# A q/k item split by ScalarE and VectorE straight from its PSUM bank, with the items' products spread in another way

## The reference

```python
mod = silu(condition) @ Wada + bada
sh_a, sc_a, gt_a, sh_m, sc_m, gt_m = jnp.split(mod, 6, axis=1)
xm = layernorm(x, g1, be1) * (1.0 + sc_a[:, None, :]) + sh_a[:, None, :]
q, k, v = split_heads(xm @ Wqkv)
attn = softmax(where(causal, q @ k.T * scale, -inf))
x = x + gt_a[:, None, :] * ((attn @ v) @ Wproj + bproj)
xm = layernorm(x, g2, be2) * (1.0 + sc_m[:, None, :]) + sh_m[:, None, :]
x = x + gt_m[:, None, :] * (gelu(xm @ W1 + b1) @ W2 + b2)
```

## Time and profile before

| | |
|---|---|
| median of 3 runs | 3148.65 us (3148.61 to 3149.07) |
| the profiled execution | 3149.18 us |
| its span, first to last instruction | 3147.5 us |
| mean granted TensorE clock | 0.999 |
| TensorE matmuls busy | 98% of the span |
| VectorE, GpSimd, ScalarE busy | 78%, 54%, 45% |

### The profile page before, as it was taken

How to read it: one execution, slowest core, us unless ns; L and a number is a source line. 1 busy time by engine, 2 the same in 40 slices (tenths; PEclk the granted TensorE clock), 3 DMA queues, 4 the chain that set the end, 5 groups by cost and what they waited for, 6 DMA issues and landing times.

```text
span 3147.5 us, 64741 instructions
## 1 busy us (share of the span) xinstructions
PE 3099.2 (98%) x22888; PEld 2417.4 (77%) x22888; DVE 2451.6 (78%) x2975; ACT 1429.7 (45%) x2876; POOL 1704.9 (54%) x1385
## 2 busy tenths in 40 slices
PE   8999999999999999999899999999999999999999
PEld 5677777777777777766688888888888888888888
DVE  5688887787888778766787878878787787878874
ACT  4355555555555555566543333333333333333333
POOL 3388888888888888888742323232322322323232
PEclk9999999999999999999999999999999999999999
DMA  7666566666656666676713222221222313222120
GB/s 251 211 191 193 170 193 183 177 188 184 194 174 187 183 177 187 181 192 178 180 41 81 57 63 68 52 80 46 74 57 63 79 41 80 57 63 67 53 67 14
DMA packets 304625, 391.81 MB, mean 124 GB/s; under 512 B 24296, under 2 KB 206088, under 8 KB 304448
## 3 DMA queue, kind: packets, MB, share of 16 engines
q1 hardware_dynamic: 292336, 371.86, 41.7%
q10 hardware_dynamic: 12112, 17.42, 1.6%
HBM read 270.66 MB, written 118.00 MB: 123 GB/s over the span
## 4 chain that ended last, share of the span: by engine, by line
PE 90%; DVE 5%; issue 2%; DMA 1%; ACT 1%; POOL 1%; SPq 0%; DVEq 0%; ACTq 0%; POOLq 0%
PE psY L1025 22%; PE psH L1013 14%; PE psA L793 9%; PE psT L847 9%; PE psH L1016 7%; PE psA L885 7%; PE psA L797 6%; PE psP L922 6%; PE psS L816 4%; DVE mx L1379 2%; PE psA L858 2%; PE psA L765 1%; DVE psS L1375 1%; PE psA L907 1%; PE psA L902 1%
## 5 line engine op out<-in xcount | busy, mean ns | idle before, releaser
L1654 POOL TENSOR_TENSOR h_l<-h_full,h_h 128x256 fp32r<-128x256 f32 x512 | 451.2, 881 | 1099.5 <-ACT h_h L1255 1099.5
L1117 ACT ACTIVATE e<-psT 128x512 f32<-128x512 f32 (+1 forms) x1202 | 605.6, 555 | 377.0 <-PE psT L847 373.6
L1379 DVE TENSOR_REDUCE mx<-psS 128x4 f32<-128x2048 f32 (+3 forms) x384 | 665.9, 1755 | 118.6 <-PE psS L816 80.5
L1252 ACT ACTIVATE h_full<-h_full,b1c 128x256 f32<-128x256 f32 x512 | 260.4, 509 | 995.1 <-DVE h_full L1555 995.1
L1013 PE MATMUL psH<-a_l,w1p_h 128*128 128x512 f32 x2048 | 547.7, 389 | 1.0 <-ACT o_sb L1125 0.8
L1555 DVE TENSOR_REDUCE h_full<-psH 128x256 f32<-128x512 f32 x512 | 346.8, 677 | 238.8 <-PE psH L1016 230.6
L1712 POOL TENSOR_TENSOR es<-e 128x512 f32<-128x512 f32 (+1 forms) x242 | 444.9, 1839 | 159.5 <-ACT e L1117 75.6
L1013 PEld LDWEIGHTS psH<-a_l,w1p_h 128*128 128x128 f32 x2048 | 384.1, 188 | 83.1 <-ACT o_sb L1125 1.0
L847 PEld LDWEIGHTS psT<-qst,kst 97*128 97x128 f32 x2404 | 349.1, 189 | 113.7 <-issue 70.2
L847 PE MATMUL psT<-qst,kst 97*128 97x256 f32 (+1 forms) x2404 | 410.4, 290 | 3.4 <-ACT e L1117 1.7
L1025 PE MATMUL psY<-w_h,h_h 128*128 128x512 f32 x1024 | 404.2, 395 | 0.8 <-POOL h_l L1654 0.8
(11 more groups left out here) (118 smaller groups left out, 4927.5 us busy)
## 6 DMA issues: line engine op xcount, KB each, us to landing
qk_split<-qk_hl SPq DMA_DIRECT2D x128, 512.0 KB, 3.6
kst<-qk_split SPq DMA_DIRECT2D x128, 256.0 KB, 3.9
qst<-qk_split SPq DMA_DIRECT2D x128, 256.0 KB, 4.1
xin<-in_x_dram SPq DMA_DIRECT2D x64, 256.0 KB, 3.6
values<-vout ACTq DMA_DIRECT2D x64, 256.0 KB, 2.4
kmx<-qk_split SPq DMA_DIRECT2D x32, 512.0 KB, 4.7
qmx<-qk_split SPq DMA_DIRECT2D x32, 512.0 KB, 5.8
kst<-qk_split SPq DMA_DIRECT2D x128, 128.0 KB, 3.9
```

Of the source, the lines that this page charges most:

```text
L1117: act.activation(e[:, s % ERING, 2 * hp:2 * hp + 2, 0:w], score_bank(s, hp, with_a)[:, :, 0:w], ACT.Exp, scale=SCALE).then_inc(sem("exp_do ...
L1252: act.activation(h_full[:, m % 4, :], h_full[:, m % 4, :], ACT.Gelu, bias=b1c[:, m:m + 1])\
L1379: reduce = dve.tensor_reduce(mx[:, part, :, qt], psS[:, :, col:col + w], AX_X, ALU.max)
L1654: return pool.tensor_tensor(dst, full, high.bitcast(F32), ALU.subtract)
```

## The change

In the bodies ScalarE's copy of a q or k item is written as float32r in the slot of the high part. VectorE then subtracts that from the bank itself and writes the low part (`a_low`, which raises `a_lo_body`). GpSimd has no part in it any more. The next q or k item, the first turn and the first item of v wait for `a_lo_body` in place of `a_copied`; the other turns and the items of v wait as before. VectorE has the new piece one step after the item's end and ahead of a piece of the maxima in the same step. `A_SHARES` changes in four of the six places: items that had 2, 8 and 2 matmuls in three steps have 4 and 8, and the item that had 5, 1, 5, 1 has 6, 0, 6, 0. So items 1, 4, 5, 7, 10 and 11 end in steps 4, 14, 18, 24, 34 and 38 (before: 5, 15, 19, 25, 35, 39). The blocks before the bodies are as they were.

```diff
-A_SHARES = ((6, 0, 6), (2, 8, 2), (6, 0, 6), (1, 5, 1, 5), (2, 8, 2), (5, 1, 5, 1)) * 2
+A_SHARES = ((6, 0, 6), (4, 8, 0), (6, 0, 6), (1, 5, 1, 5), (4, 8, 0), (6, 0, 6, 0)) * 2
 A_STORE_LAG = 2
 
-LATE_END, HIGH_LATE, LOW_LATE, STORE_LATE = 5, 2, 3, 4
+LATE_END, STORE_LATE = 5, 4
@@ a_store, SyncE
-                sp.wait_ge(sem("a_lo_done"), ia * A_NLO + n + 1)
+                if isinstance(ia, int) and ia < AHEAD:
+                    sp.wait_ge(sem("a_lo_done"), ia * A_NLO + n + 1)
+                else:
+                    sp.wait_ge(sem("a_lo_body"), (ia - AHEAD) * A_NLO + n + 1)
@@ a_turn, TensorE
-                if not alone:
+                if not alone and TURN_AFTER[k] <= A_NQK:
+                    pe.wait_ge(sem("a_lo_body"), (ia - 1 - AHEAD) * A_NLO + TURN_AFTER[k])
+                elif not alone:
                     pe.wait_ge(sem("a_copied"), (ia - 1) * A_ITEMS + TURN_AFTER[k])
@@ a_item, TensorE
+                    elif not alone and 0 < n <= A_NQK:
+                        pe.wait_ge(sem("a_lo_body"), (ia - AHEAD) * A_NLO + n)
                     else:
                         pe.wait_ge(sem("a_copied"), ia * A_ITEMS + n)
@@ a_copy, ScalarE
                     dst, src = qk_hl[:, n % QK_RING, LOW[n % 2]], psA[:, item_bank(n, alone), :]
+                    if not alone:
+                        dst = qk_hl[:, n % QK_RING, HIGH[n % 2]].bitcast(F32R)
@@ VectorE
-            def a_high(ia, n):
+            def a_low(ia, n):
 
                 if n < A_NQK:
                     dve.wait_ge(sem("a_copied"), ia * A_ITEMS + n + 1)
-                    full = qk_hl[:, n % QK_RING, LOW[n % 2]]
-                    dve.tensor_tensor(qk_hl[:, n % QK_RING, HIGH[n % 2]].bitcast(F32R), full, full, ALU.max)\
-                       .then_inc(sem("qk_hi"), 1)
+                    dve.tensor_tensor(qk_hl[:, n % QK_RING, LOW[n % 2]].bitcast(F32R), psA[:, item_bank(n, False), :],
+                                      qk_hl[:, n % QK_RING, HIGH[n % 2]], ALU.subtract).then_inc(sem("a_lo_body"), 1)
@@ body, VectorE
+                    item = ended(u, s - 1, with_a, after_a)
+                    if item:
+                        a_low(*item)
                     if r in MAX_AT:
                         d, n = MAX_AT[r]
                         if not (last and h + d >= 2):
                             max_item(u, h + d, n, with_a)
-                    item = formed(u, s, 1, HIGH_LATE, with_a, after_a)
-                    if item:
-                        a_high(*item)
@@ body, GpSimd
-                    item = formed(u, s, 1, LOW_LATE, with_a, after_a)
-                    if item:
-                        a_low(*item)
```

## The result

The changed kernel takes 3160.17 us (median of 6 runs, 3159.52 to 3160.65), the kernel before 3148.77 us in the same comparison (6 runs, 3148.28 to 3149.07): a ratio of 1.0036, with a 95% interval of 1.0024 to 1.0048. That is 11.4 us, and it lies above the 0.2% that the prediction drew as its bound, so the change makes the kernel slower. The forecast was 3157.4 us, from 3147 to 3167. The profiled execution took 3159.56 us, with a span of 3157.8.

The account below looks back on a forecast made before the run. Only TensorE's own order was taken to set the time. Terms of +0.76 us per body gave +9.1 for bodies 0 to 11, body 12 -0.4: +8.7 on the profiled 3149.18, a median of 3157.4 us, range 3147 to 3167.

Parts of the forecast that it names:

- the two waits that were named: New TensorE waits for VectorE's low part: 0.60 us at step 23's first turn, 0.68 at item 4's start in step 13.
- turn, step 23: First turn's transposes, right behind the maximum's products, must wait for the low part instead of ScalarE's copy: +0.60 us.
- item 4, step 13: Item 3's low part queues behind a join held by GpSimd's add and a statistics piece; item 4 waits: +0.68 us.
- steps 7 and 27: A low part ahead of the mask add delays the maximum's reduce, and TensorE's products wait: +0.13 us in each.
- step 11: The maximum's products waited for a reduce; the piece ahead is now shorter and never held, so the wait goes: -0.17 us.
- step 19: The last sums waited for GpSimd's add; with a 1.3 us subtract gone from before it, the wait goes: -0.29 us.
- spread of the products: Lone products leave steps 17, 19, 37, 39 (-0.06 each); four items become (4, 8, 0) (-0.02 each): together -0.32 us.
- The subtract, 0.70: VectorE's low part, reading the bank and one SBUF operand, takes 0.70 us like the mask add, unhindered by GpSimd.
- Body 12: The last body with a block has no turn and no statistics: +0.1 + 0.26 - 0.78 = -0.4 us.
- the first (the join isn't held): Step 13's wait is only 0.2 us, a body +0.3, the kernel 3151.6 us, no change; chance 0.2.
- The second, that VectorE is early everywhere: The bank's new release is covered, in step 23 too; only gains stand, -0.78 in 13 bodies, 3138.5 us; chance 0.1.
- the third, 1.155 us for the subtract: The subtract lasts as long as the old piece; four waits grow by 0.455 each, about 3180 us; chance 0.1.

Follow-up runs that it names:

- the two repairs: The changed kernel with the join of the maxima moved behind item 3's low part and the first turn moved to the end of step 25's values: 3148.47 us.
- the repaired versions: The changed kernel with step 12's statistics piece moved ahead of the join of the maxima, 3152.67 us, or with the join moved behind item 3's low part, 3152.21 us.

## Why the prediction was right

The direction, the mechanism and the size hold: the two waits that were named carry the loss, and the two repairs bring the time to 3148.47. Term by term, in us per body, for body 6; measured values are differences between starts of the same matmuls in both traces:

| step | forecast | measured |
|---|---|---|
| turn, step 23 | +0.60 | +0.66 |
| item 4, step 13 | +0.68 | +0.83 |
| steps 7 and 27 | +0.13 each | +0.11 each |
| step 11 | -0.17 | -0.22 |
| step 19 | -0.29 | -0.29 |
| spread of the products (measured: what is left) | -0.32 | -0.32 |
| sum | +0.76 | +0.88 |

- **The subtract, 0.70.** 685 ns, never held. The Trainium skill (SBUF — State Buffer, Who interferes with whom) says that a VectorE instruction with one SBUF input does not contend with GpSimd, and that one with two contends with a GpSimd instruction that reads SBUF. The traces agree on the first: 104 low parts with one such input last 0.66 to 0.69 us. They agree on the second where GpSimd adds: the join, whose two inputs are both in SBUF, takes 1.37 for 32 elements a row. Beside GpSimd's masking, which reads SBUF too, it took 0.18 where it stands behind the low part, which the page's rule doesn't lead one to expect.
- **The turn** is short by 0.06: TensorE starts 0.15 us after VectorE's end, where 0.05 was allowed, partly offset by 0.03 instead of 0.06 between ScalarE and VectorE.
- **Item 4** was forecast to start 30.49 us into the body (728.87) and starts at 30.56 (734.48 less 703.92). It was due earlier than forecast, at 29.73 instead of 29.81, since step 11 gave more. A gain ahead of a wait that another engine ends turns into more wait.
- **Steps 11 and 19.** Both waits are gone; step 11's products follow the lone one by 0.33 (728.66 to 728.99), not by the 0.38 of step 17, which had been the yardstick.
- **The spread** is worth its 0.3 here, though by itself only 0.09: inside the change the waits of steps 11 and 19 no longer stand behind it. Its row is what the others leave, so that the two -0.32 prove little. By steps, the lone products gave -0.18 (16 to 19) and -0.12 (36 to 39), against -0.12 each, and the (4, 8, 0) items about nothing, against -0.08. That these differences cancel is luck.
- **Body 12 was the mis-sized term**: -0.4 in the forecast, +0.43 measured. The forecast let it have all the gains. It never had the waits of steps 11 and 19, 0.46 of these gains: from the lone product to the last maximum of step 11 it was 0.33 us before the change too. Item 4 waits 0.19 in it (0.1 in the forecast), with no statistics piece ahead (values at 1290.46, item 4 at 1291.65). And the new spread costs it 0.15 in steps 13 to 15, beside item 4's wait, and 0.12 in 33 to 35: with the two products of step 15 gone, the maximum's products start 0.10 us after VectorE's copy of the turned maxima ends (1295.72 and 1295.82), which they have to wait for. The kernel before with the spread and the old places of the parts loses 0.13 at each of the same two places of body 12. No term of the forecast had this wait.
- **Total.** Bodies 0 to 11, with what stands ahead of them, gave +10.5 (+9.1 forecast), body 12 +0.4 (-0.4), all behind the bodies -0.6 (0 forecast; its cause is open). That is +10.3 on the span, and 1.6 more than the forecast. The other 1.1 us of the distance between 3157.4 and 3160.17 is that the median stood 0.6 above the profiled execution, where the forecast had set it 0.5 below.

Of the rivals, the first (the join isn't held) is what the repaired versions show at 3152; in the changed kernel the hold is there. The second, that VectorE is early everywhere, and the third, 1.155 us for the subtract, are ruled out by the rows on the turn and on L1371.

## What to carry to other kernels

When a buffer's release moves from one engine to the next in a chain, price the new release at each place where the buffer is wanted again, as the end of the queue ahead of it on the new engine: what stands in front of it, and what can hold that. The engine's share of busy time says nothing of this (VectorE lost 74 us of work here, and the kernel became 11 us slower), and a piece of 32 elements can carry most of the loss. Where a change has two parts, time each alone: here one alone costs 1.2% and the other, in one execution, 4.4%, and together 0.36%.

## What the runs showed that had not been expected

- A VectorE instruction with both operands in SBUF is held by its place, not by its size: the join of 32 elements a row took 0.18, 0.86 or 1.37 us, and ended 0.04 to 0.06 us after a GpSimd add wherever it was held. The 0.18 was beside GpSimd's masking, which has one input.
- The granted clock can fall to 0.53 for 3.6 us after a wait of 2.06 us, which adds some 1.2 us to its price; behind a wait of the same length in the same body the scores and values keep their full speed. Neither the length of the wait nor the step decides, since behind step 26 the clock fell in three bodies of 13 and behind step 6 in twelve. What does decide was not tried.
- Setting four transposes between the two halves of 16 values cost 0.21 us beyond the work itself. The Trainium skill (TensorEngine Tiling (Array Packing), Key Properties) says that a change of tiling mode drains the engine; the values write tiles of 32 columns and the turn 128, and the two changes that the split adds cost 0.14 and 0.07 us in this trace. Whether it is the drain, no run tells.
